# Order of a pair's shift and stack loads on SyncE, and the layout of the DRAM image of the attention operands

## The chip, the core and the metric

The kernel is one program on one core of a Trainium2 chip. The core has TensorE (PE), VectorE (DVE), ScalarE (ACT), GpSimd (POOL) and SyncE (SP), which run their own instruction lists and meet at semaphores, and 16 DMA engines that all queues share. The metric is device time in microseconds, the median of several executions.

## The reference

The input x is 2048 tokens of 128 numbers. Eight layers follow; the third, fifth, sixth and eighth hold an attention, and the rest are a state space layer, experts and a circular convolution:

```
x = x + _L0_attn_a_ref(_layernorm(x))      # state space
x = x + _L0_ffn_ref(_layernorm(x))         # 9 experts, top 2
x = x + _L0_attn_b_ref(_layernorm(x))      # local attention, window 128, and a feed-forward
x = x + _L0_ffn_ref(_layernorm(x))
x = x + _L1_attn_a_ref(_layernorm(x))      # sliding attention, window 64
x = x + _L1_ffn_ref(_layernorm(x))         # full attention, then 8 experts and a shared one
x = x + _L1_attn_b_ref(_layernorm(x))      # circular convolution with decay ("hologram")
x = x + _L1_ffn_ref(_layernorm(x))
```

Each attention has 16 heads of 8 numbers:

```
scores = jnp.einsum('blhd,bmhd->bhlm', q, k) * scale + bias
attn = jax.nn.softmax(scores, axis=-1)
ctx = jnp.einsum('bhlm,bmhd->blhd', attn, v).reshape(B, L, D)
```

## The kernel before

**Operands in parts.** `project_stage` makes q and k and splits each number into three bf16 parts (`parts`, 128 partitions = 16 heads x 8 dimensions). A score is the sum of six products of parts, so a head's operand is a stack of 6 slots x 8 dimensions = 48 rows (`ROWS`) of 2048 tokens. `Q_SLOTS` and `K_SLOTS` say which part goes into which slots. SyncE stores the parts into `image_dram` (line 819, 12 stores in each attention stage), waits until all have landed, and the stage ends. The next block loads each head's 48 rows from the image into `q_stack` and `k_stack`, three buffers deep (`STACKS`), two heads side by side (rows 0 to 47 and 64 to 111).

**Windowed stages** (`window_heads_stage`, local and sliding attention). Heads go in 8 pairs. For a pair h, PE makes the scores once to find each row's maximum (`max_units`, line 1207, 8 units w = 0 to 7; VectorE reduces them, line 1402). GpSimd splits the negated maximum into three parts, PE turns it into rows (`shift_rows`, line 1226), ScalarE copies those into `pair_rows` (line 1350), and two DMAs write them as rows 48 to 50 of the pair's q_stack: one from SyncE and one from GpSimd, a head each (`store_shift`, line 1293). Only then can PE make the scores a second time, transposed and with the maximum subtracted inside the matmul (`exp_unit`, lines 1247 and 1255, 8 units u; ScalarE takes the exponential, line 1366), and multiply by the values (`pv_step`, line 1277). Unit 0 of `exp_unit` waits for both shift DMAs.

PE's program weaves three pairs: max unit w of pair h; with w = 0 to 4 the scores 3 to 7 of pair h-2; with w = 5 to 7 the scores 0 to 2 of pair h-1; value passes at w = 0, 2, 4 and 6. So unit 0 of a pair's second scores comes right behind max unit 5 of the next pair, and max unit 0 of the pair after that, which needs a new stack, comes three max units later. `shift_rows` of a pair stands before score unit 5 (`SHIFT_UNIT`) of the pair before it.

**SyncE's program** there (lines 1449 to 1464): loads of the first pairs, then for every pair e: for e = 1 to 5 the four loads (q and k, two heads) of pair e + 2, which wait on `st_ready` until all 8 score units of pair e - 1 are made (their buffer is that pair's); then a wait for `rows_taken` (pair_rows of pair e is written) and the shift of head 0.

**Full stages** (`full_heads_stage`) work head by head in the same way with 2048 x 2048 scores; there SyncE's loop already has the shift first (lines 1106 to 1111).

Of the kernel before, what the change touches and what calls it, by code (L numbers as in the profile page):

```python
# [19 lines left out]
bf16 = mybir.dt.bfloat16  # L20
# [7 lines left out]
N_TOK = 2048  # L28
D = 128
# [5 lines left out]
HD = D // HEADS  # L35
# [13 lines left out]
SLOTS = 6  # L49
ROWS = SLOTS * HD  # L50
# [76 lines left out]
def bank(c, n, width=CHUNK):  # L127
    return c.ps[:, n * CHUNK:n * CHUNK + width]
# [602 lines left out]
def project_stage(c, w, bq=None, bk=None, bv=None, paired=False):  # L731


    nc = c.nc
# [12 lines left out]
    with nc.Block() as block:  # L747

        @block.tensor
        def _(pe):  # L750
            for n in range(2):
                for k in range(CHUNKS):
                    nc.tensor.matmul(bank(c, n * CHUNKS + k), c.proj[:, w + n, :], c.ht[:, k * CHUNK:(k + 1) * CHUNK],
                                     start=True, stop=True).then_inc(qk_ready.sem, 1)
            for t in range(TILES):
                if t % TPC == 0:
                    pe.wait_ge(*q_taken.after(2 * (t // TPC + 1)))
                ins = nc.tensor.matmul(bank(c, t // TPC)[:, (t % TPC) * P:(t % TPC + 1) * P], c.ht[:, t * P:(t + 1) * P],
                                       c.proj[:, w + 2, :], start=True, stop=True)
                if t % TPC == TPC - 1:  # L760
                    ins.then_inc(v_ready.sem, 1)

        @block.scalar
        def _(act):

            for n, (b, taken) in enumerate(((bq, q_taken), (bk, k_taken))):
                for k in range(CHUNKS):
                    cols = slice(k * CHUNK, (k + 1) * CHUNK)
                    act.wait_ge(*qk_ready.after(n * CHUNKS + k + 1))
                    for out in (c.big[:, n, cols], c.parts[:, n, 0, cols]):  # L770
                        nc.scalar.activation(out, bank(c, n * CHUNKS + k), ACT.Identity,
                                             bias=b if b is not None else 0.0).then_inc(taken.sem, 1)
            for k in range(CHUNKS):
                act.wait_ge(*v_ready.after(k + 1))
                nc.scalar.activation(c.v[:, k * TPC:(k + 1) * TPC, :].rearrange("p t d -> p (t d)"), bank(c, k),
                                     ACT.Copy).then_inc(v_taken.sem, 1)

        @block.vector
        def _(dve):
            for n, (taken, split_done) in enumerate(((q_taken, q_split), (k_taken, k_split))):  # L780
                for k in range(CHUNKS):

                    cols = slice(k * CHUNK, (k + 1) * CHUNK)
                    x, part = c.big[:, n, cols], c.parts[:, n, :, cols]
                    dve.wait_ge(*taken.after(2 * (k + 1)))
                    nc.vector.tensor_tensor(x, x, part[:, 0, :], ALU.subtract).then_inc(split_done.sem, 1)
                    dve.wait_ge(*split_done.after(SPLIT_STEPS * k + 1))
                    nc.vector.tensor_copy(part[:, 1, :], x).then_inc(split_done.sem, 1)
                    dve.wait_ge(*split_done.after(SPLIT_STEPS * k + 2))
                    nc.vector.tensor_tensor(part[:, 2, :], x, part[:, 1, :], ALU.subtract).then_inc(split_done.sem, 1)  # L790
            if bv is not None:
                dve.wait_ge(*v_taken.after(CHUNKS))
                nc.vector.tensor_tensor(c.v[:], c.v[:], bv.rearrange("p (o d) -> p o d", o=1).broadcast_to((P, TILES, D)),
                                        ALU.add)

        @block.gpsimd
        def _(pool):

            fills = [(c.k_stack[32:HALF], 1.0), (c.k_stack[HALF + 32:P], 1.0)]
            if paired:  # L800
                fills += [(c.pair_v[:], 0.0)] + [(c.pair_v[:, :, g, :, HD * (2 * g + 1):HD * (2 * g + 2)], 1.0) for g in range(2)]
            else:
                fills += [(c.v_head[:], 0.0), (c.v_head[:, :, :, HD:2 * HD], 1.0)]
            for n, (rows, value) in enumerate(fills):
                if n:
                    pool.wait_ge(*zeroed.after(n))
                pool.memset(rows, value).then_inc(zeroed.sem, 1)
            n_zeroed[0] = len(fills)

        @block.sync  # L810
        def _(sp):
            for n, (ready, slots) in enumerate(((q_split, Q_SLOTS), (k_split, K_SLOTS))):
                for half in range(N_TOK // STORE):
                    cols = slice(half * STORE, (half + 1) * STORE)
                    sp.wait_ge(*ready.after(SPLIT_STEPS * (half + 1) * STORE // CHUNK))
                    for part, where in enumerate(slots):
                        dst = c.image_dram[n, where, :, cols].rearrange("s p n -> p s n")
                        src = c.parts[:, n, part:part + 1, cols].broadcast_to((P, dst.shape[1], STORE))
                        sp.dma_start(dst, src).then_inc(stored.sem, 16)
                        n_stored[0] += 1  # L820
            sp.wait_ge(*stored.after(n_stored[0] * 16))
# [12 lines left out]
def full_heads_stage(c):  # L834

    nc = c.nc
    stack_loaded = [c.count(f"full_stack_loaded_{b}") for b in range(STACKS)]
# [6 lines left out]
    rows_taken = c.count("full_shift_rows_taken")  # L844
# [46 lines left out]
    def rows_of(stack, b, g, n, cols):  # L891

        return stack[g * HALF:g * HALF + n, b, cols]
# [62 lines left out]
    def load_half(engine, h, g):  # L956

        b = h % STACKS
        for n, stack in enumerate((c.q_stack, c.k_stack)):
            rows = c.image_dram[n, :, h * HD:(h + 1) * HD, :]  # L960
            engine.dma_start(rows_of(stack, b, g, ROWS, slice(0, N_TOK)), rows).then_inc(stack_loaded[b].sem, 16)

    def store_shift(engine, e, g):
# [4 lines left out]
    with nc.Block() as block:  # L968
# [37 lines left out]
        def _(act):  # L1006
# [7 lines left out]
            def take_rows(e):  # L1014
# [5 lines left out]
                nc.scalar.activation(c.shift_rows[:], bank(c, 2)[0:PARTS * TILES, 0:P], ACT.Copy).then_inc(rows_taken.sem, 1)  # L1020

            load_half(act, 0, 1)
            take_rows(0)
            for e in range(HEADS):
# [96 lines left out]
def window_heads_stage(c, window, biases):  # L1121

    nc = c.nc
    stack_loaded = [c.count(f"full_stack_loaded_{b}") for b in range(STACKS)]
# [6 lines left out]
    rows_taken = c.count("full_shift_rows_taken")  # L1131
# [32 lines left out]
    def rows_of(stack, b, g, n, cols):  # L1164

        return stack[g * HALF:g * HALF + n, b, cols]
# [115 lines left out]
    def load_half(engine, h, g):  # L1282

        b = h % STACKS
        head = 2 * h + g
        for n, stack in enumerate((c.q_stack, c.k_stack)):
            engine.dma_start(rows_of(stack, b, g, ROWS, slice(0, N_TOK)), c.image_dram[n, :, head * HD:(head + 1) * HD, :])\
                .then_inc(stack_loaded[b].sem, 16)

    def store_shift(engine, e, g):  # L1290

        dst = rows_of(c.q_stack, e % STACKS, g, EXP_ROWS, slice(0, N_TOK))[ROWS:EXP_ROWS]
        engine.dma_start(dst.rearrange("s (t n) -> s t n", n=P), c.pair_rows[g * PARTS * TILES:(g + 1) * PARTS * TILES, :])\
            .then_inc(shift_loaded[g].sem, 16)

    with nc.Block() as block:
# [39 lines left out]
        def _(act):  # L1336
# [7 lines left out]
            def take_rows(e):  # L1344
# [5 lines left out]
                nc.scalar.activation(c.pair_rows[:], bank(c, SHIFT_BANK)[0:2 * PARTS * TILES, 0:P], ACT.Copy).then_inc(rows_taken.sem, 1)  # L1350

            load_half(act, 0, 1)
            take_rows(0)
            for e in range(PAIRS):
# [93 lines left out]
        @block.sync  # L1448
        def _(sp):
            def load_stacks(h):  # L1450

                if h >= STACKS:
                    sp.wait_ge(*st_ready.after((h - STACKS + 1) * EXP_UNITS))
                for g in range(2):
                    load_half(sp, h, g)

            load_half(sp, 0, 0)
            for h in range(1, STACKS):
                load_stacks(h)
            for e in range(PAIRS):  # L1460
                if 1 <= e < PAIRS - STACKS + 1:
                    load_stacks(e + STACKS - 1)
                sp.wait_ge(*rows_taken.after(e + 1))
                store_shift(sp, e, 0)

    biased.passed(len(biases))
    for b in range(STACKS):
# [411 lines left out]
def hybrid_stack(nc, i, out, layers="abcdefgh"):  # L1879
    with ExitStack() as ctx:  # L1880
        c = Core(nc, ctx)
# [57 lines left out]
            ("L0_attn_a_ln_gamma", D), ("L0_attn_a_ln_beta", D), ("L0_attn_b_bv", D), ("L0_attn_b_bo", D),  # L1939
            ("L0_attn_b_b2", D), ("L1_attn_b_decay", 1), ("L1_attn_b_gate", 1))}  # L1940
        c.ps = ctx.enter_context(nc.psum_tensor("ps", [P, 8 * CHUNK], fp32))
        c.image_dram = nc.dram_tensor("image_dram", (2, SLOTS, D, N_TOK), bf16).ap()
        c.keys_dram = nc.dram_tensor("keys_dram", (2, 2 * D), fp32).ap()

        constants_stage(c)
# [134 lines left out]
```

## Time and profile before

| | us |
|---|---|
| median of 3 runs | 3097.5 |
| lowest and highest | 3094.97, 3098.13 |
| the profiled execution | 3101.99 |
| its span, from first to last instruction | 3100.2 |
| PE busy | 2612.1 (84%) |
| DVE busy | 2228.2 (72%) |
| ACT busy | 1521.7 (49%) |
| mean granted TensorE clock | 0.904 |

The busy shares are averages over stages with different limits. The local stage lies at about 393 to 612 us of the span, the sliding one at 960 to 1162, the two full ones at 1196 to 1900 and 2177 to 2880. What bounds a stage is read from its own waits: for each idle time the profile names the instruction or DMA that came last. "SPq" is SyncE issuing a DMA; a DMA's data moves later.

### The profile page before, as it was taken

Reading aid. Unit: us, or ns where it says so; the run is one execution under the profiler, and the core shown is the slowest. Engines: PE = TensorE matmul, PEld = TensorE weight load, DVE = VectorE, ACT = ScalarE, POOL = GpSimd, SP = SyncE. Lnnn points to the kernel's source line nnn. Section 1 sums busy time; section 2 is a strip of 40 time slices with the busy share of each in tenths; the row PEclk is TensorE's granted clock in tenths of the full one; section 3 lists DMA queues with packets and bytes.
Section 4 is the critical chain, followed back from the end, with each engine's and each line's share of the span. In section 5 each row is a group of like instructions: output and inputs, shape, how many; then the busy total and the mean of one; then the engine's idle time right before and its main releaser. Section 6 shows DMA issues by size and latency. Waiting matters only on the chain. (4 is left out here: it accounts for less than half of the span.)

```text
span 3100.2 us, 48788 instructions
## 1 busy us (share of the span) xinstructions
PE 2612.1 (84%) x18006; PEld 1299.6 (42%) x18006; DVE 2228.2 (72%) x5400; ACT 1521.7 (49%) x1907; POOL 333.1 (11%) x610
## 2 busy tenths in 40 slices
PE   6799736779994564999999997995699999999799
PEld 3588613458882341122222223884112222221488
DVE  6644565444446536999999994556799999998454
ACT  2222223432222331477777776321177777778522
POOL 4100220020002002000000001003100000000100
PEclk8799868879996785799999998997599999999899
DMA  2000031000003103000000000000300000000000
GB/s 53 22 22 21 0 123 33 13 15 20 16 14 112 33 23 112 9 16 20 22 22 22 22 12 11 16 20 2 112 12 22 22 22 22 22 22 2 11 26 24
DMA packets 60361, 88.94 MB, mean 29 GB/s; under 512 B 12006, under 2 KB 37484, under 8 KB 60156
## 3 DMA queue, kind: packets, MB, share of 16 engines
q1 hardware_dynamic: 58188, 84.03, 8.1%
q8 instruction: 125, 2.05, 0.3%
q10 hardware_dynamic: 432, 1.57, 0.2%
q0 software_dynamic: 1536, 0.63, 0.2%
q14 instruction: 80, 0.66, 0.1%
HBM read 57.93 MB, written 26.22 MB: 27 GB/s over the span
## 5 line engine op out<-in xcount | busy, mean ns | idle before, releaser
L1062 DVE TENSOR_REDUCE pair_mx<-ps 128x1 f32<-128x512 f32 x2048 | 1270.9, 683 | 43.0 <-PE ps L904 38.7
L1034 ACT ACTIVATE prob<-ps 128x1024 f32<-128x1024 f32 x1024 | 990.1, 1021 | 249.4 <-PE ps L939 247.6
L904 PE MATMUL ps<-k_stack,q_stack 48*128 48x512 bf16 x2048 | 643.9, 405 | 93.9 <-DMA k_stack<-image_dram 52.0
L953 PE MATMUL ps<-prob,v_head 128*32 128x512 f32 x4096 | 547.3, 606 | 1.3 <-ACT prob L1034 1.0
L904 PEld LDWEIGHTS ps<-k_stack,q_stack 48*128 48x128 bf16 x2048 | 148.7, 93 | 941.1 <-DVE pair_mx L1062 843.9
L1741 DVE TENSOR_TENSOR hid<-silu,ps 128x512 f32<-128x512 f32 x360 | 246.0, 685 | 369.7 <-PE ps L1678 250.7
L1710 ACT ACTIVATE silu<-ps 128x512 f32<-128x512 f32 x360 | 214.5, 597 | 574.6 <-PE ps L1678 566.6
L939 PE MATMUL ps<-q_stack,k_stack 51*128 51x512 bf16 x2048 | 438.8, 383 | 8.5 <-ACT prob L1034 5.3
L1690 PEld LDWEIGHTS ps<-wd,hid 128*128 128x128 f32 (+1 forms) x2880 | 364.4, 191 | 27.6 <-issue 2.6
L1690 PE MATMUL ps<-wd,hid 128*128 128x128 f32 (+1 forms) x2880 | 369.1, 275 | 0.7 <-DVE hid L1741 0.3
L1678 PE MATMUL ps<-ht_part,wg_part 128*128 128x512 f32 (+1 forms) x1080 | 335.8, 420 | 16.8 <-PEq L299 14.8
L1678 PE MATMUL ps<-ht_part,wu_part 128*128 128x512 f32 (+1 forms) x1080 | 310.4, 396 | 2.4 <-DVE hid L1741 2.4
L1402 DVE CUSTOM_DVE_ANT_0 ps<-ps,mask 128x256 f32<-128x256 f32 (+2 forms) x512 | 180.2, 419 | 140.8 <-PE ps L1207 139.1
L1678 PEld LDWEIGHTS ps<-ht_part,wu_part 128*128 128x128 f32 (+1 forms) x1080 | 199.7, 185 | 56.9 <-DVE hid L1741 5.1
L1366 ACT ACTIVATE prob<-ps 128x1024 f32<-128x1024 f32 (+1 forms) x128 | 115.3, 917 | 177.3 <-PE ps L1255 177.3
L1678 PEld LDWEIGHTS ps<-ht_part,wg_part 128*128 128x128 f32 (+1 forms) x1080 | 182.4, 188 | 44.0 <-issue 15.0
L1725 DVE SCALAR_TENSOR_TENSOR x<-ps,cw_now,x 128x128 f32<-128x128 f32 x544 | 152.9, 343 | 54.7 <-PE ps L1690 37.3
L1247 PE MATMUL ps<-half_k,half_ident 64*128 64x512 bf16 (+1 forms) x512 | 80.4, 397 | 86.9 <-DMA q_stack<-pair_rows 86.3
L1207 PE MATMUL ps<-k_stack,q_stack 48*128 48x256 bf16 (+2 forms) x512 | 55.6, 304 | 93.7 <-DMA k_stack<-image_dram 54.1
L939 PEld LDWEIGHTS ps<-q_stack,k_stack 51*128 51x128 bf16 x2048 | 105.6, 95 | 62.4 <-ACT prob L1034 45.5
L953 PEld LDWEIGHTS ps<-prob,v_head 128*32 128x32 f32 x4096 | 81.0, 108 | 120.4 <-issue 117.2
L1085 POOL CAST shift<-rowmax 128x16 bf16<-128x16 f32 x32 | 6.3, 195 | 1009.0 <-DVE rowmax L1066 1009.0
(186 smaller groups left out, 1761.6 us busy)
## 6 DMA issues: line engine op xcount, KB each, us to landing
q_stack<-image_dram SPq DMA_DIRECT2D x92, 192.0 KB
k_stack<-image_dram SPq DMA_DIRECT2D x92, 192.0 KB
image_dram<-parts SPq DMA_DIRECT2D x16, 768.0 KB, 4.3
image_dram<-parts SPq DMA_DIRECT2D x16, 512.0 KB, 5.2
image_dram<-parts SPq DMA_DIRECT2D x16, 256.0 KB, 5.2
wg<-in_L_ffn_Wg_dram SPq DMA_DIRECT2D x18, 176.0 KB, 2.3
wu<-in_L_ffn_Wu_dram SPq DMA_DIRECT2D x18, 176.0 KB, 2.5
wd<-in_L_ffn_Wd_dram SPq DMA_DIRECT2D x18, 128.0 KB, 2.4
```

The source lines that it names most:

```text
L904: nc.tensor.matmul(max_bank(n), rows_of(c.q_stack, b, g, ROWS, slice(t * P, (t + 1) * P)), rows_of(c.k_stack, b, g, ROWS, slice(k * CHUNK, ...
L939: ins = nc.tensor.matmul(bank(c, 2 * (u % 2) + g), rows_of(c.k_stack, b, g, EXP_ROWS, slice(kb * P, (kb + 1) * P)), rows_of(c.q_stack, b, ...
L953: ins = nc.tensor.matmul(out, c.v_head[:, e % 2, kb, :], unit, start=(kb == 0), stop=(kb == TILES - 1), skip_group_check=True)
L1034: nc.scalar.activation(c.prob[:, u % P_UNITS, :], c.ps[:, 2 * (u % 2) * CHUNK:2 * (u % 2) * CHUNK + UNIT], ACT.Exp, scale=scale).then_inc( ...
L1062: nc.vector.reduce_max(mx[:, w:w + 1], max_bank(n), AX.X).then_inc(max_taken.sem, 1)
L1366: nc.scalar.activation(probs, scores, ACT.Exp, scale=scale).then_inc(exp_done.sem, 1)
L1402: ins = nc.vector.tensor_tensor_reduce(scores, scores, c.mask32[:, window, P - back:WIDE], 1.0, LOWEST, ALU.add, ALU.max, accum_out=mx[:, ...
L1678: ins = nc.tensor.matmul(bank(c, at + unit % 2)[0:m], w[:, p, u, j * P:j * P + m], c.ht_part[:, v, k * CHUNK:(k + 1) * CHUNK], start=(a == ...
L1690: ins = nc.tensor.matmul(bank(c, 4 + k % 2)[:, t * P:(t + 1) * P], c.hid[0:m, k % 2, j, t * P:(t + 1) * P], c.wd[0:m, p, j, :], start=(j = ...
L1710: nc.scalar.activation(c.silu[0:m, unit % 2, :], bank(c, unit % 2)[0:m], ACT.Silu).then_inc(silu_ready.sem, 1)
L1725: ins = nc.vector.scalar_tensor_tensor(tile, out, c.cw_now[:, p, k * TPC + t:k * TPC + t + 1], tile, ALU.mult, ALU.add)
L1741: nc.vector.tensor_tensor(c.hid[0:m, k % 2, j, :], c.silu[0:m, unit % 2, :], bank(c, 2 + unit % 2)[0:m], ALU.mult).then_inc(hid_ready.sem, 1)
```

## The change

Two things. In `window_heads_stage`, SyncE's loop now waits for `rows_taken` and sends the shift of pair e first, and then issues the loads of pair e + 2. And `image_dram` has the shape (2, 128, 6, 2048) instead of (2, 6, 128, 2048): the six slots of one dimension lie one behind the other, so the 48 rows of a head are one run of 192 KB. The rows of a stack come in another order (dimension first, then slot), for q and k alike, so each score is the sum of the same 48 products. Stores and loads in all four attention stages take the new shape.

```
@@ project_stage
-                        dst = c.image_dram[n, where, :, cols].rearrange("s p n -> p s n")
+                        dst = c.image_dram[n, :, where, cols]
@@ full_heads_stage, load_half
-            rows = c.image_dram[n, :, h * HD:(h + 1) * HD, :]
+            rows = c.image_dram[n, h * HD:(h + 1) * HD].rearrange("d s n -> (d s) n")
@@ window_heads_stage, load_half
-            engine.dma_start(rows_of(stack, b, g, ROWS, slice(0, N_TOK)), c.image_dram[n, :, head * HD:(head + 1) * HD, :])\
-                .then_inc(stack_loaded[b].sem, 16)
+            rows = c.image_dram[n, head * HD:(head + 1) * HD].rearrange("d s n -> (d s) n")
+            engine.dma_start(rows_of(stack, b, g, ROWS, slice(0, N_TOK)), rows).then_inc(stack_loaded[b].sem, 16)
@@ window_heads_stage, SyncE
             for e in range(PAIRS):
+                sp.wait_ge(*rows_taken.after(e + 1))
+                store_shift(sp, e, 0)
                 if 1 <= e < PAIRS - STACKS + 1:
                     load_stacks(e + STACKS - 1)
-                sp.wait_ge(*rows_taken.after(e + 1))
-                store_shift(sp, e, 0)
@@ hybrid_stack
-        c.image_dram = nc.dram_tensor("image_dram", (2, SLOTS, D, N_TOK), bf16).ap()
+        c.image_dram = nc.dram_tensor("image_dram", (2, D, SLOTS, N_TOK), bf16).ap()
```

SyncE before, in the local stage, from the shift of pair 0 to the first load of pair 4; `full_shift_rows_taken` is `rows_taken`, `full_scores_ready` is `st_ready`, and each row is one DMA:

```order
L1293 DMA q_stack<-pair_rows 3x16x128 [waits full_shift_rows_taken]
L1287 DMA q_stack<-image_dram 48x1x2048 [waits full_scores_ready]
L1287 DMA k_stack<-image_dram 48x1x2048
L1287 DMA q_stack<-image_dram 48x1x2048
L1287 DMA k_stack<-image_dram 48x1x2048
L1293 DMA q_stack<-pair_rows 3x16x128 [waits full_shift_rows_taken]
L1287 DMA q_stack<-image_dram 48x1x2048 [waits full_scores_ready]
```

The same place in the changed kernel:

```order
L1293 DMA q_stack<-pair_rows 3x16x128 [waits full_shift_rows_taken] x2
L1288 DMA q_stack<-image_dram 48x2048 [waits full_scores_ready]
L1288 DMA k_stack<-image_dram 48x2048
L1288 DMA q_stack<-image_dram 48x2048
L1288 DMA k_stack<-image_dram 48x2048
L1293 DMA q_stack<-pair_rows 3x16x128 [waits full_shift_rows_taken]
L1288 DMA q_stack<-image_dram 48x2048 [waits full_scores_ready]
```

Pair 1's shift moved ahead of pair 3's four loads, pair 2's ahead of pair 4's, and so on to pair 5; the loads have two dimensions instead of three on the stack's side. On PE, VectorE and GpSimd nothing moves, on ScalarE only the form of its two loads at each stage's start changes.

## Rows read from the trace of the kernel before

**Rows 1.** The page, costliest groups: count, busy us and mean ns, idle time before.

```profile
L1062 DVE TENSOR_REDUCE pair_mx<-ps 128x1 f32<-128x512 f32 x2048 | 1270.9, 683 | 43.0 <-PE ps L904 38.7
```

**Rows 2.** Who PE waited for, whole kernel: us in total, times, longest.

```profile
PE ps L1247 <- DMA q_stack<-pair_rows: 86.3, 10, 9.1
PE ps L1207 <- DMA k_stack<-image_dram: 54.1, 2, 27.7
...
PE ps L904 <- DMA k_stack<-image_dram: 52.0, 2, 26.6
...
PE ps L939 <- DMA q_stack<-shift_rows: 1.4, 2, 0.7
```

**Rows 3.** Who SyncE's queue waited for, whole kernel.

```profile
SPq L1287 <- PE ps L1255: 191.7, 10, 21.9
```

**Rows 4.** Timeline of SyncE, local stage, one transition: start us, us, what.

```profile
481.20 0.75 SPq L1287 DMA_DIRECT2D q_stack<-image_dram  x1
...
484.25 0.78 SPq L1293 DMA_DIRECT2D q_stack<-pair_rows  x1
```

**Rows 5.** Timeline of ScalarE, the same transition.

```profile
477.15 0.27 ACT L1350 ACTIVATE pair_rows<-ps 96x128 bf16<-96x128 f32 x1 [1.35 <-PE ps L1226]
```

**Rows 6.** Timeline of PE, the same transition, to the next pair's max unit 0.

```profile
481.00 0.38 PE L1207 MATMUL ps<-k_stack,q_stack 48*128 48x256 bf16 x4
489.79 1.03 PE L1247 MATMUL ps<-half_k,half_ident 64*128 64x512 bf16 x4 [8.40 <-DMA q_stack<-pair_rows]
...
495.72 0.34 PE L1207 MATMUL ps<-k_stack,q_stack 48*128 48x128 bf16 x4 [0.40 <-DVE pair_mx L1402]
```

**Rows 7.** Timeline of SyncE, the shift of pair 6, without loads ahead.

```profile
577.18 0.76 SPq L1293 DMA_DIRECT2D q_stack<-pair_rows  x1
```

**Rows 8.** Timeline of PE at pair 6's first score unit.

```profile
580.73 0.38 PE L1207 MATMUL ps<-k_stack,q_stack 48*128 48x256 bf16 x4
580.95 0.59 PE L1247 MATMUL ps<-half_k,half_ident 64*128 64x512 bf16 x4
```

**Rows 9.** Stretches: us, busy of five engines, PEclk, DMA share, GB/s.

```profile
393.00:411.00 18.00, 0.81 (x8) 0.62 (x6) 13.08 (x20) 2.27 (x5) 2.12 (x3) 0.65 0.95 350
487.00:488.00 1.00, 0.00 (x0) 0.00 (x0) 0.00 (x0) 0.00 (x0) 0.00 (x0) 0.50 0.37 147
```

**Rows 10.** The page, DMA issues: count, KB each, median us to landing.

```profile
wg<-in_L_ffn_Wg_dram SPq DMA_DIRECT2D x18, 176.0 KB, 2.3
```

**Rows 11.** Line 1583, weight loads: issue time on SyncE in ns, min/median/max.

```profile
L1583 SPq DMA_DIRECT2D wg<-in_L_ffn_Wg_dram x18: 332/344/422, 91.8 to 881.9; - x18
```

**Rows 12.** Timeline of PE, local stage, max units 5 and 0 after pair 1.

```profile
441.82 0.61 PE L1207 MATMUL ps<-k_stack,q_stack 48*128 48x256 bf16 x4 [0.97 <-DVE pair_mx L1402]
...
446.89 0.34 PE L1207 MATMUL ps<-k_stack,q_stack 48*128 48x128 bf16 x4 [0.24 <-DVE pair_mx L1402]
```

**Rows 13.** Timeline of PE, sliding stage, the same two units, undisturbed and steady.

```profile
1004.25 0.50 PE L1207 MATMUL ps<-k_stack,q_stack 48*128 48x192 bf16 x4 [0.83 <-DVE pair_mx L1402]
...
1008.33 0.45 PE L1207 MATMUL ps<-k_stack,q_stack 48*128 48x128 bf16 x4
...
1015.87 0.33 PE L1207 MATMUL ps<-k_stack,q_stack 48*128 48x192 bf16 x4
...
1029.94 0.32 PE L1207 MATMUL ps<-k_stack,q_stack 48*128 48x128 bf16 x4
```

**Rows 14.** Timeline of SyncE, first stack load of local and sliding stage.

```profile
411.75 0.90 SPq L1287 DMA_DIRECT2D q_stack<-image_dram  x1
...
978.43 0.87 SPq L1287 DMA_DIRECT2D q_stack<-image_dram  x1
```

**Rows 15.** Timeline of PE, first max unit of local and sliding stage.

```profile
421.50 0.50 PE L1207 MATMUL ps<-k_stack,q_stack 48*128 48x128 bf16 x4 [27.69 <-DMA k_stack<-image_dram]
...
986.88 0.45 PE L1207 MATMUL ps<-k_stack,q_stack 48*128 48x128 bf16 x4 [26.41 <-DMA k_stack<-image_dram]
```

## Prediction

> **What bounds the kernel now.** I read four views, in this order. The page's costliest groups show that the two full attention stages hang on VectorE: 2048 row maxima of 683 ns, 1271 us in all with 43 us of idle time before them [rows 1]. Nothing in the change touches VectorE's work. The list of PE's waits comes next, because PE feeds every other engine in attention [rows 2]. Its largest entry is not a compute engine: PE waited 86.3 us in 10 pieces, at most 9.1 us each, for a DMA that writes a pair's shift rows into the query stack (pair_rows to q_stack). The next ones for DMA are the first stack load of each attention stage, 54.1 us for the two windowed stages and 52.0 us for the two full ones (most of that is the projection and the stores before them, which stay). In the full stages the shift costs PE only 1.4 us in all: there SyncE already sends it before the loads.
>
> Then the same moment on three engines, in the local stage around 481 us. ScalarE writes pair_rows at 477.15 [rows 5], so the shift could leave at about 477.4. SyncE does not send it: it stands at the load of the pair after next, which waits until PE has made all scores of the running pair (10 such waits in the kernel, 191.7 us [rows 3]). At 481.20 it issues four loads of 192 KB and only at 484.25 the shift [rows 4]. PE, out of other work since 481.00, resumes at 489.79, 8.40 us later [rows 6]. So 4 us are the place in SyncE's program and nearly 5 us are the four loads that lie ahead of 12 KB of shift in the same queue.
>
> That queue is slow for a reason of its own. While the stores run, the 16 DMA engines are 0.95 busy and move 350 GB/s; while only stack loads run, 0.37 busy and 147 GB/s [rows 9]. 0.37 is 6 of 16 engines: the load's source has 6 slots as its outermost dimension, the stores have 128 partitions there.
>
> **Part 1, the shift first (window_heads_stage, SyncE).** Three DMAs of SyncE's program per pair swap places: one shift, and the loads behind it. Nothing is added. The shift is sent after pair_rows is written, at about 477.4 instead of 484.25, and four loads of that pair move behind it; since the shift's condition was true 3.8 us before the loads' condition, the loads are not delayed (0.8 us of issue fit into that gap). Does the shift land in time? The same DMA without loads ahead is in the trace: pair 6's was issued at 577.18 [rows 7], and PE's first score matmul of that pair ran at 580.95, right behind its previous work and with no wait shown [rows 8]. So it lands within 3.8 us of issue; 477.4 + 3.8 = 481.2, which is where PE gets there. The 10 waits fall to about 0. GpSimd's half of the shift already takes that course.
>
> What is late next? For a steady pair I measure from the max matmuls of unit 5 to those of unit 0 of the next pair, which holds the whole wait: before 481.00 to 495.72, 14.72 us [rows 6]. Three max units lie between, and VectorE sets their pace: in the first pair, where nothing is waited for, the same stretch took 441.82 to 446.89, 5.07 us [rows 12], although PE's clock was at its lower level there (a matmul group of 1.03 us at 489.79 against 0.59 at 580.95 [rows 6, 8]; the granted clock in such a gap is 0.50, the 1.2 GHz level [rows 9]). The extra value pass of a steady pair fits into PE's idle share. Saved: 14.72 - 5.07 = 9.65 us, more than the 8.40 us of the wait, since PE no longer falls to the lower clock in the gap and has not to climb back. Five times: **48 us**. The sliding stage the same way: 1015.87 to 1029.94 is 14.07, the undisturbed first pair 1004.25 to 1008.33 is 4.08 [rows 13], 9.99 saved if nothing else is late.
>
> **Part 2, the loads.** Something else may be late: the stack of the next pair must be there at that unit 0, 5.07 us (local) or 4.08 us (sliding) after the loads are issued. Before, four loads took until about 489.5, 8.3 us (the shift behind them let PE go at 489.79). With the new image the source is 48 rows in one run, a shape of two dimensions like the weight loads. The nearest rows: a weight load of 176 KB from 128 rows lands 2.3 us after issue [rows 10], and SyncE takes 0.34 us to issue it [rows 11]; four stack loads take 481.20 to 484.25, 0.76 us each [rows 4]. Lower end: first data about 1.8 us after issue (2.3 less 0.5 for the bytes), then 4 x 192 KB at 350 GB/s, 2.2 us, with all four issued by then: landed at 4.0 to 4.2 us. Upper end, if issue stays at 0.76 us: last one issued at 2.3, plus 2.3 and some queueing, 4.6 to 5.3 us. I take 4.2, because the shape is that of the weight loads: no wait in the local stage, 0.2 to 0.4 us in the sliding one, so 9.6 x 5 = **48 us** there. The upper end costs 0.2 us x 5 local and 1.0 x 5 sliding more, 6 us.
>
> The Trainium skill has a rule for this, in "DMA: Bandwidth & Descriptors", section "Why a DMA increments its semaphore by 16 and not by 1": a DMA is spread over the largest number of engines up to 16 that divides the slowest dimension of both sides. By it 6 and 48 give 6 engines and 48 and 48 give 16, so the loads would be 16/6 = 2.7 times as fast; the 0.37 and 0.95 of this trace agree. If it did not hold for the new shape, rival 1 below would be the result.
>
> The four attention stages also begin with these loads. In the local stage the first is issued at 411.75 and PE starts at 421.50, 9.75 us; in the sliding one 978.43 to 986.88, 8.45 us [rows 14, 15]; the two full stages lie between; mean 9.1. Four loads are needed there too, two from each of SyncE and ScalarE. With 4.2 us as above, 4.9 us saved each, **20 us** in four; with the upper end, 5.2 us, 16 us. The other loads of the full stages are not waited for at all: nothing saved, nothing lost.
>
> **Part 3, the stores.** 48 stores write the same bytes in pieces of the same 2 KB; only the addresses change (slots 4 KB apart instead of 512 KB, partitions 24 KB instead of 4 KB). They now move 350 GB/s over the whole 18 us of a stage's start [rows 9], all engines busy, so they cannot gain; 0, with 2 us either way.
>
> **Sum.** 48 + 48 + 20 = 116 us. From the profiled execution's 3102.0: 2986. The median of the runs is 4.5 us lower, 3097.5 - 116 = **2981.5**. Bounds: upper ends of the loads (6 + 4) and stores (2) give 2994; a full 10 us at each of the ten places and 2 us from the stores give 2975.
>
> **Rivals.**
> Rival 1, the layout does not speed the loads (the change does half of what it says): they stay on 6 engines. Against it: 0.37 against 0.95 matches the outermost dimensions. Then the shift is no longer late but the stack is: landed 8.3 us after issue, needed at 4.1 to 5.1, so PE waits 3.2 to 4.2 us at the same ten places, and falls to the lower clock again, 1.3 us each (9.65 less the wait of 8.40). Gain 9.8 - 3.7 - 1.3 = 4.8 us x 10 = 48, nothing at the stage starts: 3050.
> Rival 2, the loads become 16-wide but land late, at 5.8 to 6.3 us after issue, because four of them and GpSimd's shift meet on the same engines: PE waits 1.5 us more at 14 places, 21 us: 3003.
> Rival 3, slower than before: the new addresses are bad for the memory. Each DMA engine would write 2 KB pieces 24 KB apart and later read one run, so that many engines could meet in the same part of memory. Price: at a third of 350 GB/s the 18 us of stores become 54, 36 more in each of four stages, 144 in all against 116 gained: 3126. It decides from 29 us a stage, below some 134 GB/s. Against it: the old layout, with 512 KB between slots, shows no such loss.
>
> **How the numbers follow.** Forecast 0.80 (2975 to 2994), rival 2 0.09, rival 1 0.08, rival 3 0.03. For 8 in 10 the range takes the forecast's bounds and part of rival 2: 2972 to 3004. Of the measurement's 0.2% (6 us) every case but rival 3 is far clear: faster 0.96, within 0.01, slower 0.03.
>
> **What would show it.** In the profile after: no wait of PE for pair_rows over 1 us; shift DMAs on SyncE ahead of four loads; a DMA share near 1 at over 300 GB/s in the 2 us after each group of loads; issue of a stack load at about 0.35 us; PE at 4.2 us after the first load of a stage; from unit 5 to unit 0 of the next pair about 5.1 us (local) and 4.4 us (sliding) instead of 14.7 and 14.1; granted clock 1.00 through the pairs. The forecast is wrong if PE waits for k_stack at a pair's first max unit (rivals 1 and 2), or if the stores' stretch is longer than 18 us (rival 3).

## The result and the profile after

The changed kernel took 3021.2 us (median of 4, 3019.5 to 3023.0) against 3097.8 us: ratio 0.975, 95% interval 0.973 to 0.977. It gains 76.6 us where 116 were forecast, and lies outside the range. The profiled execution took 3023.0 us.

The list of PE's waits of the changed kernel (us in total, times, longest), to be held against [rows 2]:

```profile
PE ps L1207 <- DMA k_stack<-image_dram: 75.1, 12, 24.3
...
PE ps L904 <- DMA k_stack<-image_dram: 47.6, 2, 24.6
```

The 86.3 us for the shift are gone. But L1207 now waits for k_stack 12 times, not 2. Ten of these waits are new: 1.98 to 2.72 us at the five places of the local stage, 3.05 to 3.23 us at the five of the sliding one. PE's first max unit of a pair (start us, us, what, wait before it), with one unit 5 ahead of it in each stage; the rows up to 494.33 are of the local stage, the last three of the sliding one. The rows at 417.46 and 942.40 answer to [rows 15], the local ones to [rows 6], the last two to [rows 13]:

```profile
417.46 0.50 PE L1207 MATMUL ps<-k_stack,q_stack 48*128 48x128 bf16 x4 [24.26 <-DMA k_stack<-image_dram]
...
458.78 0.34 PE L1207 MATMUL ps<-k_stack,q_stack 48*128 48x128 bf16 x4 [2.41 <-DMA k_stack<-image_dram]
...
476.86 0.34 PE L1207 MATMUL ps<-k_stack,q_stack 48*128 48x128 bf16 x4 [2.18 <-DMA k_stack<-image_dram]
...
486.80 0.38 PE L1207 MATMUL ps<-k_stack,q_stack 48*128 48x256 bf16 x4
487.02 0.59 PE L1247 MATMUL ps<-half_k,half_ident 64*128 64x512 bf16 x4
...
493.90 0.50 PE L1207 MATMUL ps<-k_stack,q_stack 48*128 48x128 bf16 x4 [2.72 <-DMA k_stack<-image_dram]
494.33 1.93 PE L1277 MATMUL ps<-prob,pair_v 128*32 128x128 f32 x32
...
942.40 0.45 PE L1207 MATMUL ps<-k_stack,q_stack 48*128 48x128 bf16 x4 [23.45 <-DMA k_stack<-image_dram]
...
1020.32 0.33 PE L1207 MATMUL ps<-k_stack,q_stack 48*128 48x192 bf16 x4
...
1027.09 0.45 PE L1207 MATMUL ps<-k_stack,q_stack 48*128 48x128 bf16 x4 [3.21 <-DMA k_stack<-image_dram]
```

The score matmul at 487.02 stands right behind unit 5: the shift is in time. From unit 5 to unit 0 it is 486.80 to 493.90, 7.10 us, against 14.72 before and 5.07 forecast. In the sliding stage it is 1020.32 to 1027.09, 6.77 us, against 14.07 before and 4.4 forecast. After the wait of 2.72 us the value matmuls take 1.93 us, so PE falls to the lower clock (the granted clock is 0.64 in the stretch of 493 to 494 below); after the wait of 2.18 us they take 1.08 us.

SyncE at the same transition, to be held against [rows 4]:

```profile
483.24 0.72 SPq L1293 DMA_DIRECT2D q_stack<-pair_rows  x1
487.00 0.31 SPq L1288 DMA_DIRECT2D q_stack<-image_dram  x1
487.35 0.42 SPq L1288 DMA_DIRECT2D k_stack<-image_dram  x1
487.81 0.42 SPq L1288 DMA_DIRECT2D q_stack<-image_dram  x1
488.27 0.42 SPq L1288 DMA_DIRECT2D k_stack<-image_dram  x1
```

The order is as meant, and issue takes 0.31 to 0.42 us instead of 0.75. PE may go on only 6.90 us after the first issue. Where that time goes is in the stretches (us, busy of PE, PEclk, DMA share, GB/s), to be held against [rows 9]:

```profile
487.00:488.00 1.00, 0.83 (x12) 1.00 0.14 25
488.00:489.00 1.00, 0.86 (x23) 1.00 0.96 270
489.00:490.00 1.00, 1.00 (x23) 1.00 1.03 160
490.00:491.00 1.00, 1.00 (x18) 1.00 1.05 205
491.00:492.00 1.00, 0.18 (x4) 1.00 0.90 135
492.00:493.00 1.00, 0.00 (x0) 1.00 0.04 4
493.00:494.00 1.00, 0.10 (x4) 0.64 0.02 4
```

All engines are busy, as forecast, but they move 135 to 270 GB/s, not 350. The bytes need 4.0 us, 197 GB/s on average; the first flow 0.9 us after the issue, and PE is released 2.0 us after the last.

### The profile page after: what moved, and what is told of

It reads as the page before. It is cut to its first block and busy times, and to the rows that moved or that the text cites. A ratio compares the mean times of both kernels' runs of the same rounds, so it can differ in the third digit from the quotient of the medians.

```text
span 3021.2 us, 48788 instructions
## 1 busy us (share of the span) xinstructions
PE 2605.4 (86%) x18006; PEld 1292.0 (43%) x18006; DVE 2228.3 (74%) x5400; ACT 1519.9 (50%) x1907; POOL 333.1 (11%) x610
## 5 line engine op out<-in xcount | busy, mean ns | idle before, releaser
L1207 PE MATMUL ps<-k_stack,q_stack 48*128 48x256 bf16 (+2 forms) x512 | 53.8, 296 | 111.8 <-DMA k_stack<-image_dram 75.1
L1609 POOL TENSOR_TENSOR wg_part<-wg,wg_part 128x352 fp32r<-128x352 f32 (+1 forms) x36 | 30.1, 837 | 681.4 <-ACT wg_part L1602 681.4
```

## The experiments

Theory A: loads into 48 partitions are capped at about 200 GB/s by the side of SBUF that they land on. Theory B: reading one run of DRAM is slow. Theory C: they meet other traffic. Gains below are against the kernel before on the same chip.

| kernel | us | gain | ratio, interval |
|---|---|---|---|
| the change | 3021.2 | 76.6 | 0.975, 0.973 to 0.977 |
| shift first only | 3065.0 | 35.5 | 0.989, 0.987 to 0.991 |
| layout only | 3069.0 | 31.5 | 0.990, 0.989 to 0.992 |
| 8 DMA engines | 3047.3 | 55.2 | 0.983, 0.981 to 0.984 |
| loads in alternating order | 3011.6 | 90.8 | 0.971, 0.970 to 0.973 |
| second head from ScalarE | 3009.2 | 91.5 | 0.971, 0.969 to 0.972 |
| four stacks | 3004.3 | 96.1 | 0.969, 0.967 to 0.971 |
| fills behind the casts | 3016.3 | 86.2 | 0.972, 0.971 to 0.974 |
| fills on VectorE | 3029.9 | 70.8 | 0.977, 0.975 to 0.980 |
| four stacks, GpSimd's fills at the back | 2993.2 | 109.2 | 0.965, 0.963 to 0.967 |
| four stacks, VectorE's fills | 3009.1 | 91.6 | 0.970, 0.969 to 0.972 |
| four stacks, fills in pieces | 2969.5 | 131.6 | 0.958, 0.956 to 0.959 |

**The loads by themselves.** A program of DMAs alone: in each phase three groups of four loads of 192 KB, each group waited for.

```diff
+ for k in range(4):
+     sp.dma_start(m["t_run"][0:48, k], rows(4 * r + k)).then_inc(...)
...
+     at = 64 * (k % 2)
+     sp.dma_start(m["t_alternate"][at:at + 48, k], rows(4 * r + k)).then_inc(...)
...
+     sp.dma_start(m["t_straddle"][40:88, k], rows(4 * r + k)).then_inc(...)
```

> A program of loads alone (no layer is computed, the output is the input): groups of four loads of 48 rows of 4 KB, 768 KB a group, three times each, nothing else on the queues. Groups: run (source one run, destination partitions 0 to 47), alternate (0 to 47 and 64 to 111 in turn), straddle (partitions 40 to 87), six (the old image: source six pieces of 8 rows, 0 to 47), padded (rows 4352 bytes apart, 0 to 47), wide (two loads of 96 rows, partitions 16 to 111), two (two loads from SyncE to 0 to 47 beside two from ScalarE to 64 to 111). Theory A, the destination's ports are the limit (48 partitions below 64 are reached by half of the ports): run and padded alike at 190 to 215 GB/s with the engines near 1.0 busy; straddle faster, 250 or more; wide and two at 300 to 380; six at 0.37 busy and 150. Theory B, a source in one run is slow to read: padded and six faster per engine than run, straddle and wide as slow as run, near 200. Theory C, it is contention with other traffic in the full kernel: run reaches 350 here.

SyncE's timeline of it, one row a phase:

```profile
63.50 15.39 SPq L1912 DMA_DIRECT2D t_run<-one_run  x12
83.60 12.85 SPq L1917 DMA_DIRECT2D t_alternate<-one_run  x12
100.44 11.46 SPq L1921 DMA_DIRECT2D t_straddle<-one_run  x12
115.01 20.81 SPq L1926 DMA_DIRECT2D t_six<-six_runs  x12
141.63 14.67 SPq L1930 DMA_DIRECT2D t_padded<-padded_rows  x12
161.29 10.43 SPq L1934 DMA_DIRECT2D t_wide<-one_run  x6
175.76 12.20 SPq L1939 DMA_DIRECT2D t_two<-one_run  x6
193.12 0.41 SPq L1870 DMA_DIRECT2D out_dram<-x  x1
```

From a phase's start to the next, divided by three, a group takes 6.70 us into partitions 0 to 47 (run), 5.61 when every second load goes to 64 to 111 (alternate), 4.86 into 40 to 87 (straddle), 8.87 with the old image (six), 6.55 from rows with a gap of 256 bytes between them in DRAM (padded), 4.8 as two loads of 96 rows into 16 to 111 (wide), 5.8 from two queues into the two halves (two). Nothing else runs, and the slow case is nearly as slow as in the kernel (6.90): C falls. Other rows of DRAM change little (padded), and run, alternate and straddle read the same rows of DRAM: B falls. Where the bytes land changes much: A stands. The steady part of a group in two phases (us, GpSimd, PEclk, DMA share, GB/s):

```profile
65.00:68.00 3.00, 0.00 (x0) 1.00 1.06 199
...
102.00:104.00 2.00, 0.00 (x0) 1.00 1.00 311
```

The same 16 engines are busy in both, for 199 and 311 GB/s. Over a whole group of 787 KB the DMA shares of its stretches of 1 us add up to 4.16 and 2.75 us: 189 and 286 GB/s while the engines are busy, 1.5 times. One part of theory A's expectation failed: wide and two were to reach 300 to 380 GB/s. Their first groups add up to 2.90 and 3.09 us, 271 and 255 GB/s, so 96 partitions at once were no faster than the 48 of straddle, and why stays open. The Trainium skill states the rule on where the bytes land in "SBUF — State Buffer", section "Door 1: The DMA port swizzle (why `[64,N]` ≈ `[32,N]`)": what counts is how many of SBUF's 16 ports the partitions reach; 0 to 63 reach 8, and by its table of ports 40 to 87 reach 12. The 1.5 times of the trace agree with 12 ports against 8.

**One half of the change at a time.** First the order of SyncE's program alone, with the old image:

```diff
             for e in range(PAIRS):
+                sp.wait_ge(*rows_taken.after(e + 1))
+                store_shift(sp, e, 0)
                 if 1 <= e < PAIRS - STACKS + 1:
                     load_stacks(e + STACKS - 1)
-                sp.wait_ge(*rows_taken.after(e + 1))
-                store_shift(sp, e, 0)
```

> The kernel before with the order on SyncE alone: the shift ahead of the loads, the image as it was. The loads then stay at 0.37 of the DMA engines and land about 8.3 us after issue, while the next pair's max unit 0 wants them after 5.1 us (local) or 4.1 us (sliding). My theory (the two parts add up, and the loads become the wait that is left): no wait of PE for pair_rows, ten waits of 3 to 4.5 us for k_stack, gain 10 x 4.8 = 48 us, 3050. Rival (the order alone brings nearly all of the 77 us measured for both, since a late stack is hidden by VectorE's backlog): ten waits of at most 2.7 us, as in the changed kernel, 3035 or less.

It gained 35.5 us, 12 less than expected. The wait moved on to the stack, and the ten waits are 5.2 us on average where 3 to 4.5 were expected:

```profile
464.72 0.50 PE L1207 MATMUL ps<-k_stack,q_stack 48*128 48x128 bf16 x4 [4.48 <-DMA k_stack<-image_dram]
...
508.08 0.50 PE L1207 MATMUL ps<-k_stack,q_stack 48*128 48x128 bf16 x4 [6.25 <-DMA k_stack<-image_dram]
```

Then the image alone, with the loads still ahead of the shift (the change without this edit):

> The changed kernel with SyncE's old order: loads ahead of the shift, image in one run per head. My theory: the shift now stands behind four loads that take 4 us of data (4 x 192 KB at the 200 GB/s seen in the changed kernel) instead of 5.4 and are issued in 1.9 us instead of 3.05, so it lands 6 to 7 us after the first load's issue instead of 8.4 to 9; ten waits for pair_rows of about 6.5 us instead of 8.6: 20 to 25 us, and 2.6 us at each of the four stage starts, 10 us: 3063 to 3068. Rival (the layout gives nothing beyond the stage starts, the loads move no faster than before in the middle of a stage): 3085 or more.

The gain of 31.5 us is near the 30 to 35 expected. PE still waits for the shift, less long than in [rows 2]:

```profile
PE ps L1247 <- DMA q_stack<-pair_rows: 62.8, 10, 6.7
```

The parts give 67 us apart and 77 together. That each takes away something that hides the other's gain would fit, but the difference of 10 us is little more than the intervals of the gains (about 5 us either way each), so it is not shown.

**Eight engines.** The image has a seventh slot that holds nothing, so a load's 48 rows are eight runs of six.

```diff
-            rows = c.image_dram[n, head * HD:(head + 1) * HD].rearrange("d s n -> (d s) n")
+            rows = c.image_dram[n, head * HD:(head + 1) * HD]
...
-        c.image_dram = nc.dram_tensor("image_dram", (2, D, SLOTS, N_TOK), bf16).ap()
+        c.image_dram = nc.dram_tensor("image_dram", (2, D, SLOTS + 1, N_TOK), bf16).ap()[:, :, 0:SLOTS, :]
```

> The changed kernel, with the image in DRAM widened to seven slots of which the seventh is never written or read. A head's 48 rows then are eight runs of six rows, so a load's descriptors go to 8 of the 16 DMA engines instead of all. Theory A (the loads are held to about 200 GB/s by where they land, partitions 0 to 47 or 64 to 111): eight engines of 22 to 25 GB/s each carry 180 to 200 GB/s, so the loads land within 0.4 us of the changed kernel's 6.4 to 7.1 us after the first issue; DMA share near 0.5 during the loads instead of near 1.0 at the same GB/s; 3020 to 3028 us. Rival (the number of source engines sets the rate, as the prediction had it): the rate halves, each of ten starts and the four stage starts lose 3 us or more: 3055 us or more.

3047 lies between the two numbers and meets neither. At the local stage's start (415.00 is 1.8 us after the first issue):

```profile
416.00:417.00 1.00, 0.00 (x0) 0.50 0.52 209
417.00:418.00 1.00, 0.00 (x0) 0.50 0.51 180
418.00:419.00 1.00, 0.00 (x0) 0.50 0.51 172
419.00:420.00 1.00, 0.00 (x0) 0.50 0.50 201
```

Half the engines carry a mean of 190 GB/s; the changed kernel's sixteen carry 226 in its stretches 413 to 417 (279, 213, 213, 201). So each of the sixteen moves less than each of the eight does: the engines are not what caps the changed kernel, yet eight are just below that cap. The other difference is issue time: 0.64 to 0.82 us a load for this three-dimensional source, not 0.31 to 0.42. PE's waits for k_stack are 143.0 us in all instead of 122.7, which is nearly the whole loss of 21 us; how it splits between rate and issue was not measured.

**Both partition halves at once.** With a pair's loads as q, q, k, k of its two heads:

```diff
-                for g in range(2):
-                    load_half(sp, h, g)
+                b = h % STACKS
+                for n, stack in enumerate((c.q_stack, c.k_stack)):
+                    for g in range(2):
+                        ...
+                        sp.dma_start(rows_of(stack, b, g, ROWS, slice(0, N_TOK)), rows).then_inc(...)
```

> The changed kernel, with a pair's four loads issued in the order q of head 0, q of head 1, k of head 0, k of head 1 (in the local and sliding stages), so that two loads in flight go to different partition halves. Theory A, with the DMA-only program's 5.61 us a group against 6.70 us: the ten waits of TensorE on k_stack shrink from about 2.6 us to about 1.5 us each, 11 us in all, 3010 us. Rival (what holds the loads is traffic that meets them, GpSimd's shift and others, or the address order in DRAM): the ten waits stay 2.0 to 3.2 us, 3020 to 3022 us.

The gain grew by 14 us (11 expected), but the waits explain less than half of it. The ten are 21.4 us in all instead of 27.4 (15 expected): 1.29 to 2.09 us in the local stage, 1.77 to 3.18 in the sliding one. The local stage also ran at a higher granted clock (0.96 against 0.81 in 492 to 510 us); where the rest came from was not traced. Two of the waits:

```profile
457.76 0.34 PE L1207 MATMUL ps<-k_stack,q_stack 48*128 48x128 bf16 x4 [1.29 <-DMA k_stack<-image_dram]
...
473.66 0.34 PE L1207 MATMUL ps<-k_stack,q_stack 48*128 48x128 bf16 x4 [1.59 <-DMA k_stack<-image_dram]
```

The other way, with the second head's loads issued by ScalarE:

```diff
+                    if u == EXP_UNITS - 1 and e < PAIRS - STACKS:
+                        load_half(act, e + STACKS, 1)
```

> The changed kernel, with the second head's two loads of each of the ten later pairs issued by ScalarE, behind its last piece of probabilities of the pair before, while SyncE issues the first head's: loads for partitions 0 to 47 and for 64 to 111 then run side by side. Theory A (each partition half is reached at about 200 GB/s, both halves together at more; the DMA-only program had 5.80 us a group this way and 6.70 us one after the other): the ten waits shrink by about 0.9 us each, 3012 us; less, and up to no gain, if ScalarE comes to its two issues later than SyncE does. Rival (the cap is on the whole traffic): the ten waits stay, 3021 us.

It gave 15 us where 9 were expected, and the ten waits fell from 27.4 us to 13.9. Part of that is issue and not the halves: the four loads of the pair at 487 us begin to be issued within 0.4 us here (486.92 to 487.32), in the changed kernel within 1.3 us. The Trainium skill says in "SBUF — State Buffer", section "Can I just issue two DMAs to hit both halves?", that two concurrent DMAs, one at partition 0 and one at partition 64, gain only 6%, since they serialize. In the program of loads alone a group into both halves took 5.61 us from one queue and 5.8 from two, against 6.70, which is 13 to 16% less time; for loads of this shape the measurement decides.

**Four stacks.** If only the landing is late, a fourth stack must remove all ten waits.

```diff
-STACKS = 3
+STACKS = 4
```

> The changed kernel with four stack buffers instead of three, so that each pair's four loads are issued a whole pair earlier and have some 18 us instead of 4 to 5. It measures what the late landing costs. My theory: the ten waits for k_stack of 2.0 to 3.2 us go, and with them the falls to PE's lower clock; from max unit 5 to unit 0 of the next pair takes the 5.1 and 4.1 us of the prediction instead of 6.5 and 7.2; gain 10 x 2.7 = 27 us and up to 5 more by the clock: 2989 to 2995. The full stages do not change. Rival (what is missing to the prediction lies elsewhere, in VectorE or in the value passes, and takes the wait's place): 3010 or more, with new waits on PE.

3004, not 2989 to 2995, but the ten waits are gone:

```profile
PE ps L904 <- DMA k_stack<-image_dram: 55.2, 2, 28.9
PE ps L1207 <- DMA k_stack<-image_dram: 55.1, 2, 27.6
```

```profile
471.49 0.38 PE L1207 MATMUL ps<-k_stack,q_stack 48*128 48x256 bf16 x4
...
476.28 0.34 PE L1207 MATMUL ps<-k_stack,q_stack 48*128 48x128 bf16 x4 [0.40 <-DVE pair_mx L1402]
```

Unit 5 to unit 0 is 4.79 us; the forecast had 5.07. The four waits at the stages' starts are 110.3 us instead of 95.3, which is why the kernel missed its expectation. The cause of the longer waits is in the projection, where GpSimd fills k_stack with ones (first row, changed kernel; the last two are four stacks) while VectorE casts (middle rows, changed kernel):

```profile
381.00 10.65 POOL L807 MEMSET k_stack<- 32x6144 bf16 x2 [3.24 <-POOLq L299]
```

```profile
385.14 1.35 DVE L788 CAST parts<-qk 128x512 bf16<-128x512 f32 x1
...
387.86 4.08 DVE L788 CAST parts<-qk 128x512 bf16<-128x512 f32 x1
```

```profile
382.08 14.06 POOL L807 MEMSET k_stack<- 32x8192 bf16 x2 [3.24 <-POOLq L299]
...
390.64 5.78 DVE L788 CAST parts<-qk 128x512 bf16<-128x512 f32 x1
```

A cast alone takes 0.43 us. Each of these ends 0.2 to 0.3 us after a fill does, and the stores wait behind it. By the Trainium skill ("SBUF — State Buffer", section "Who interferes with whom") a cast on VectorE can contend with GpSimd for a port pair that the two share, and whoever issues first holds it for the whole instruction; the trace agrees.

**Where the fills go.** Five kernels move them. On GpSimd behind the last cast, with three stacks (the fills of pair_v now come first):

```diff
+                if n == before_stacks:
+                    pool.wait_ge(*k_split.after(SPLIT_STEPS * CHUNKS))
```

> The changed kernel, with GpSimd's two fills of k_stack in the projection stage (10.65 us from its start, beside which VectorE's casts take up to 4.08 us instead of 0.43 us) moved behind VectorE's last cast, under the 19 us of stores; all else as it is. Theory (the fills hold the casts, the casts hold the first stores): the stores start about 4 us earlier in each of four projection stages, 16 us in all, 3005 us. Rival 1 (ScalarE's pieces set the pace, the casts were hidden): no change, 3021 us. Rival 2 (the fills now end after the stores): half of the gain, 3013 us.

All casts take 0.43 us, but the gain grew by 10 us only, near rival 2: the fills now end last (start us, us):

```profile
400.94 10.48 POOL L810 MEMSET k_stack<- 32x6144 bf16 x2 [15.34 <-DVE parts L790]
```

With four stacks, the same place of the fills, alternating loads, and the first stack waited for before the others are issued:

```diff
             load_half(sp, 0, 0)
+            sp.wait_ge(*stack_loaded[0].after(LOADS * 16))
             for h in range(1, STACKS):
```

> Four stacks, fills behind the casts, loads in alternating order, and SyncE waits for the first pair's (in the full stages the first head's) stack before it issues the other loads. Theory: the ten waits go (31 us, as the ends of the units with four stacks showed), the starts gain 4 us each at four places from the casts and up to 1 us each from the first loads being alone: 2970 to 2976 us. Rival: the longer fills (14 us) now end behind the stores and give back 2 to 4 us at each of four starts: 2985 to 2992 us.

Near the rival's number. The stores' traffic is at 48 GB/s in 404 to 406 us, the fills end at 411.4 and the loads start at 411.7.

On VectorE instead, with three stacks, and with four and the rest as in the last one:

```diff
+            for rows in (c.k_stack[32:HALF], c.k_stack[HALF + 32:P]):
+                nc.vector.memset(rows, 1.0)
```

> The changed kernel (three stacks), with the two fills of k_stack in the projection stage issued by VectorE behind its last cast and before it adds the values' bias, instead of by GpSimd ahead of the casts. With the fills on GpSimd behind the casts the stores ended 4 us earlier but the loads were issued only when the fills ended (411.4 us against 407.7 us). Theory (casts held by fills at the front; fills too long at the back): VectorE's two fills of 6144 elements in a row take 2 to 6 us each and end under the stores, the loads are issued 4.1 us earlier at four places, 16 us in all: 3005 us. Rival (the fills on VectorE take 6 us or more each and end behind the stores): 3010 us or more.

> Four stacks, fills on VectorE behind the casts, loads in alternating order, SyncE waits for the first stack before it issues the others. Against the same kernel with GpSimd's fills (2993 us), where traffic of the stores ended at 404.2 us and the fills at 411.4 us in the local layer, the loads can be issued 7 us earlier at each of four places: 2965 us. Rival (VectorE's longer fills end behind the stores too): 2975 to 2985 us.

Both are slower than their counterparts, by 15 and 18 us: the rivals hold, and the second kernel is 24 us beyond its rival's range. The rows give VectorE 5.18 us a fill with 1.3 us of idle time ahead of each, but from one fill's start to the next it is 6.49 us, and GpSimd needs 5.3. VectorE adds the bias only then:

```profile
401.14 5.18 DVE L792 MEMSET k_stack<- 32x6144 bf16 x1 [1.33 <-issue]
407.63 5.18 DVE L792 MEMSET k_stack<- 32x6144 bf16 x1 [1.32 <-issue]
412.82 2.29 DVE L795 TENSOR_TENSOR v<-v,row_L_attn_b_bv 128x2048 f32<-128x2048 f32 x1
```

At last in eight pieces, among the later casts, all else as in the kernel of 2993 us:

```diff
-            fills += [(c.k_stack[32:HALF], 1.0), (c.k_stack[HALF + 32:P], 1.0)]
+            fills += [(c.k_stack[r:r + 32, b], 1.0) for r in (32, HALF + 32) for b in range(STACKS)]
...
-                    pool.wait_ge(*k_split.after(SPLIT_STEPS * CHUNKS))
+                    pool.wait_ge(*q_split.after(SPLIT_STEPS * CHUNKS // 2))
```

> As the kernel with four stacks, alternating loads and GpSimd's fills behind the casts (2993 us), but the fills are eight pieces of 32 x 2048, and GpSimd begins them when the first two casts of the queries are done, so that they run between and beside the later casts. Theory (a cast waits for the end of the fill that runs when it starts, so a piece of 1.8 us costs it little): the stores start as early as with the fills at the back (386.8 us in the local layer), VectorE ends some 2 us later than there and still ahead of the stores' end, the fills end near 404 us, and the loads are issued when the stores land, 6 to 7 us earlier at each of four places: 2965 to 2970 us. Rival (the pieces and the casts hold each other on and on, and the later stores wait for them): 2980 us or more.

2969.5 us, the fastest of all and as expected. The four waits at the stages' starts are 78.3 us in all. Beside the fills one cast is held for 1.50 us, the others take 0.66; in the local stage the fills end at 405.6, the stores near 408.3, and the loads follow at once:

```profile
389.80 15.80 POOL L810 MEMSET k_stack<- 32x2048 bf16 x8 [4.61 <-DVE parts L790]
```

```profile
408.88 0.33 SPq L1292 DMA_DIRECT2D q_stack<-image_dram  x1
```

## Why the prediction was wrong, step by step

**The shift first: right.** No wait for pair_rows is left, the loads were not delayed by it, and issue fell to 0.31 to 0.42 us as taken.

**What is late next: the question was right, one term was not.** The step that failed is "first data about 1.8 us after issue (2.3 less 0.5 for the bytes), then 4 x 192 KB at 350 GB/s, 2.2 us". Measured: 0.9 us to the first bytes, 4.0 us of bytes, 2.0 us from the last byte to PE, 6.9 us where the step had 4.0 (and the sum took 4.2). The 350 GB/s came from stores that read 128 partitions; the loads write 48, and the program of loads alone shows the same rate there. That is 1.8 us of the 2.9 missed; the other 1.1 us is the fixed part, 2.9 us and not the 1.8 taken from a weight load. Even the upper end, 5.3 us, was below it, since it only varied the issue. Rival 2 named loads that are 16 wide and land late, but its 5.8 to 6.3 us were short as well, and its cause, GpSimd's shift on the same engines, is not needed: the program of loads alone is as slow without it. Rival 1's price was too low too: the shift first with loads on 6 engines came in at 3065 us in the experiment, not at 3050.

**The ten starts: mechanism right, size off.** 96 us were forecast. The gain of 76.6 less 10.8 at the stages' starts leaves 66, and the ten k_stack waits that appeared are 75.1 - 47.7 = 27.4 us (47.7 being the two stage starts, 24.26 and, at 942.40 in the sliding stage, 23.45). 66 and 27 are 93: had the stacks been there in time, the term would have held. The sum had no wait in the local stage and 0.2 to 0.4 us in the sliding one; measured were 1.98 to 2.72 and 3.05 to 3.23 us. Four stacks confirm it: 4.79 us where 5.07 were forecast, and since that kernel gained 96.1 us although its four starts waited 4.2 us longer than before the change, the ten places gave 100 us. Of the 39 us that the forecast missed, 27 are these waits, 9 the stages' starts, and 3 are unaccounted for.

**The stage starts: 10.8 us for 20.** The four waits were 106.1 us [rows 2] and are 95.3. Local: 411.10, when the first load is issued, to 417.46, so 6.4 us instead of 4.2. In the other three it is 5.5, 8.0 and 5.7 us, the mean 6.4: the same term, four times.

**The stores: right.** They move 379 GB/s in 394 to 410 us. From the first store's issue to the stage's first load it is 392.68 to 411.10, 18.4 us, as before (393.35 to 411.75 [rows 14]).

**The layout's factor.** 16 of 16 engines are busy (share 0.96 to 1.05) and so the Trainium skill's rule on engine counts, which the prediction cites, holds. But the loads got from 147 to some 200 GB/s, 1.4 times and not 2.7: another limit came first. No row of the prediction shows it, but the kernel before has one that could have warned. At its start four DMAs of 192 KB copy the mask from 64 partitions into 64 (`half_k`); in a stretch of them the engines are 0.86 busy and move 188 GB/s, not 350, though whether the reading or the writing side holds them is not shown (us, busy of the five engines, PEclk, DMA share, GB/s):

```profile
47.00:48.00 1.00, 1.00 (x2) 0.23 (x1) 1.00 (x1) 0.00 (x0) 1.00 (x1) 0.50 0.86 188
```

## What to carry to other kernels

A rate is only good for transfers with the same two ends: before a rate of stores is used for loads, look for a row with the same number and place of partitions. A range must vary the term that the sum rests on, the rate here, not only the small one beside it. If a load must land within a few microseconds, one more buffer removes the question, but look what else grows with the buffer: here its fill, which held another engine's casts.

## What the runs showed of the hardware

- Four loads of 192 KB take 6.70 us into partitions 0 to 47, 5.61 alternating with 64 to 111, and 4.86 into 40 to 87, with the same engines and bytes. Two loads of 384 KB into 16 to 111 take 4.8 us, no less.
- A load whose source has two dimensions is issued by SyncE in 0.31 to 0.42 us (longer behind many other loads, up to 1.65), with three in 0.64 to 0.82.
- A 0.43 us cast on VectorE took up to 5.78 us beside a fill of 7 us on GpSimd; against fills of 2 us it took 0.66 us mostly. The subtractions around it kept their 0.69 us in either case.
- Two fills of 32 x 6144 bf16 on VectorE start 6.49 us apart, though each row reads 5.18 us; GpSimd's take 5.3 us.
